# A small clear of an unused tile ahead of every indirect scatter on the queue of GpSimd, with a reordered preparation and a rewritten last layer norm

## The reference

```
x = x + layernorm(attn_block(layernorm(x)))
x = x + layernorm(moe(layernorm(x)))

attn_block: rms_norm, q/k/v, normalised q and k, 16 heads of 8, bias by distance bucket,
            causal softmax, Wo, residual, rms_norm, relu(z @ W1) @ W2, residual
moe:        probs = softmax(x @ router_w.T) over 8 experts; top 2 of them
            h = silu(x @ gate_w[e].T) * (x @ up_w[e].T)        # 352 wide
            y = sum over the token's 2 experts of  prob_e * (h @ down_w[e].T)
layernorm:  (x - mean) / sqrt(var + 1e-5)
```

## Time and profile before

| | |
|---|---|
| median of 3 runs | 629.49 us (626.6 to 630.55) |
| the profiled execution | 628.14 us |
| its span, first to last instruction | 626.1 us |
| PE busy | 544.4 us (87%) |
| ACT, DVE, POOL busy | 391.5, 377.7, 321.9 us |
| granted clock of PE, mean | 0.95 |

### The profile page before, as it was taken

How to read it: one execution, slowest core, us unless ns; L and a number is a source line. 1 busy time by engine, 2 the same in 40 slices (tenths; PEclk the granted TensorE clock), 3 DMA queues, 4 the chain that set the end, 5 groups by cost and what they waited for, 6 DMA issues and landing times.

```text
span 626.1 us, 13770 instructions
## 1 busy us (share of the span) xinstructions
PE 544.4 (87%) x4607; PEld 399.1 (64%) x4607; DVE 377.7 (60%) x1083; ACT 391.5 (63%) x865; POOL 321.9 (51%) x336
## 2 busy tenths in 40 slices
PE   7987899899998998997998999499758689999992
PEld 5763456456565554654565667489658689999950
DVE  6636484966966849988668866227434146555335
ACT  3458899888878888778888774244423144544415
POOL 4023546555458875278955472633454734444426
PEclk9887999999999999999999999889998789999997
DMA  8765323213223332135356212210213102321064
GB/s 198 106 140 135 102 76 120 79 33 102 77 87 101 98 104 76 41 118 131 122 159 147 66 37 54 57 31 15 61 56 85 53 27 69 90 60 31 21 268 135
DMA packets 48117, 55.86 MB, mean 89 GB/s; under 512 B 7821, under 2 KB 42384, under 8 KB 45889
## 3 DMA queue, kind: packets, MB, share of 16 engines
q1 hardware_dynamic: 43728, 46.52, 27.4%
q0 software_dynamic: 4320, 8.47, 4.3%
HBM read 37.12 MB, written 18.29 MB: 89 GB/s over the span
## 4 chain that ended last, share of the span: by engine, by line
PE 60%; DVE 15%; ACT 9%; issue 5%; another core or an unknown queue 5%; POOL 2%; DMA 2%; DVEq 1%; ACTq 0%; POOLq 0%; SPq 0%
PE SC L814 13%; PE OA L688 9%; PE OA L824 8%; PE M L729 5%; PE M L765 4%; ACT arena L933 4%; PE SC L670 3%; PE SC L674 2%; DVE SS L1220 2%; PE M L604 2%; PE SC L680 2%; PE M L623 1%; PE M L654 1%; PE M L795 1%
## 5 line engine op out<-in xcount | busy, mean ns | idle before, releaser
L933 ACT ACTIVATE arena<-SC 128x1024 f32<-128x1024 f32 x160 | 161.7, 1039 | 13.2 <-PE SC L675 11.0
L814 PE MATMUL SC<-arena 128*128 128x128 f32 (+1 forms) x852 | 111.4, 283 | 0.9 <-DVE arena L1401 0.9
L814 PEld LDWEIGHTS SC<-arena 128*128 128x128 f32 (+1 forms) x852 | 104.0, 191 | 1.4 <-DVE arena L1401 1.1
L1620 POOL DMA_INDIRECT slots<-XBA,IDX x64 | 71.9, 1123 | 56.4 <-DVE IDX L1345 39.6
L688 PE MATMUL OA<-arena 128*32 128x256 f32 (+1 forms) x1536 | 90.7, 355 | 5.4 <-DVE arena L410 2.8
L1393 DVE TENSOR_TENSOR arena<-arena,SC 128x256 f32<-128x256 f32 (+1 forms) x142 | 43.7, 348 | 84.6 <-remote 26.9
L824 PE MATMUL OA<-arena 128*128 (+1 forms) x426 | 64.2, 289 | 31.4 <-DVE arena L1393 12.5
L824 PEld LDWEIGHTS OA<-arena 128*128 128x128 f32 (+1 forms) x426 | 56.4, 202 | 34.5 <-issue 34.5
L1626 POOL DMA_INDIRECT ytok<-YSA,XGA x39 | 38.7, 992 | 61.0 <-ACT YSA L1036 57.0
L688 PEld LDWEIGHTS OA<-arena 128*32 128x32 f32 x1536 | 39.4, 110 | 44.4 <-issue 23.0
L409 POOL TENSOR_TENSOR arena<-arena 128x512 f32<-128x512 f32 x32 | 42.6, 1332 | 35.1 <-ACT arena L933 34.5
(11 more groups left out here) (220 smaller groups left out, 1063.9 us busy)
## 6 DMA issues: line engine op xcount, KB each, us to landing
arena<-parts SPq DMA_DIRECT2D x90, 192.0 KB
parts<-arena SPq DMA_DIRECT2D x16, 384.0 KB
arena<-ytok SPq DMA_DIRECT2D x8, 512.0 KB, 6.9
XGA<-slots SPq DMA_DIRECT2D x39, 65.0 KB
arena<-slots SPq DMA_DIRECT2D x32, 65.0 KB
X<-in_L_attn_x SPq DMA_DIRECT2D x4, 512.0 KB, 5.1
arena<-toe SPq DMA_DIRECT2D x16, 128.0 KB, 6.1
out<-X SPq DMA_DIRECT2D x8, 256.0 KB, 2.3
```

What stands on the lines that cost most here:

```text
L814: mm = pe.matmul(SC[0:n, r % 2, 512 * m + P * c:512 * m + P * (c + 1)], WSEL[s % 4][:, I * m + i0:I * m + i0 + n], XGT[r % 2], start=True, ...
L933: act.activation(EB[u], SC[:, n % 2, :], ACT.Exp).then_inc(exp_done, 1)
L1620: pool.indirect_dma_start(out=slots_d.ap(), out_offset=bass.IndirectOffsetOnAxis(ap=IDX[b // 2 % 2][:, k, T * r + t:T * r + t + 1], axis=0 ...
```

## The change

1. `put` and, for the last four batches, `scatter` issue `pause()` ahead of each indirect DMA: POOL clears IDLE, a tile of 128x128 float32 that nothing reads, and waits for that by `link`. That is one clear for each of the 71 puts, ahead of the wait for its result, and one for each of 32 scatter DMAs.
2. Preparation: `spread_cm` multiplies all 128 rows (CMW, cleared by DVE first) in place of 16; ACT takes the exponential of CF ahead of `xar(1)` and that of the first half of the table ahead of the last copy of batch 1; there are fewer dummy matmuls.
3. Last stage: PE adds the halves of 5 batches only, POOL of batches 1 and 4, DVE of batch 7. The inverse root starts from a logarithm and an exponential on ACT (`final_seeds`) and gets one Newton step on POOL, for the last two batches on DVE. Residuals and stores are dealt out in another order.

```diff
+        IDLE = sb("IDLE", [P, P])
+        CMW = EB[UNITS - 1][:, 3 * P:4 * P]
...
+        BY_POOL, BY_VECTOR = (1, 4), (7,)
+        BY_TENSOR = [b for b in range(NB) if b not in BY_POOL + BY_VECTOR]
+        OUT_POOL, OUT_VECTOR = (0, 1, 2, 4), (3, 7, 5, 6)
...
-            for b in (*range(NB - 2), NB - 1, NB - 2):
+            for b in (0, 1, 3, 2, 4, 7, 5, 6):
                 store(sp, b)
...
-                    mm = pe.matmul(CMB[:, h, :], IDN[0:H, h:h + 1].broadcast_to([H, P]), CMR[:, :], start=True, stop=True)
+                    mm = pe.matmul(CMB[:, h, :], IDN[:, h:h + 1].broadcast_to([P, P]), CMW, start=True, stop=True)
...
             for i in range(2):
-                keep_busy(3)
+                keep_busy(2)
                 pre_qk(1, i)
-            keep_busy(5)
+            keep_busy(2)
...
-            for b in range(NB):
+            for b in BY_TENSOR:
                 pe.wait_ge(yt_in[b], 16)
...
-            xar(1)
-            for k in range(3):
-                pre_copy(1, k)
             act.wait_ge(bias_in[0], 16 * (P // COPIES + 1))
             act.activation(CF[:, :], CF[:, :], ACT.Exp).then_inc(tab_exp, 1)
+            xar(1)
+            for k in range(2):
+                pre_copy(1, k)
             exp_table(0)
+            pre_copy(1, 2)
...
+            act.preload_act_table_set("natural_log_exp_and_others")
+            def final_seeds(q):
+                y = RSR[:, 0, 2 * T * q:2 * T * (q + 1)]
+                act.wait_ge(f_stat, 2 * q + 2)
+                act.activation(y, MV[:, 2 * T * q:2 * T * (q + 1), 1], ACT.Ln, bias=FEPS[:, 0:1]).then_inc(f_seed, 1)
+                act.wait_ge(f_seed, 2 * q + 1)
+                act.activation(y, y, ACT.Exp, scale=-0.5).then_inc(f_seed, 1)
...
+            final_seeds(0)
+            final_norm(0)
+            final_seeds(1)
+            final_norm(1)
+            final_norm(2)
+            final_seeds(2)
+            final_norm(3)
+            final_norm(4)
+            final_seeds(3)
+            final_norm(5)
+            final_norm(6)
...
+            dve.memset(CMW, 0.0)
...
                 for k in range(2):
+                    if b >= NB - 4:
+                        pause()
                     pool.indirect_dma_start(out=slots_d.ap(), out_offset=bass.IndirectOffsetOnAxis(ap=IDX[b // 2 % 2][:, k, T * r + t:T * r + t + 1], axis=0),
                                             in_=XB[r][:, t, k, :], in_offset=None).then_inc(scattered[r], 16)
+            def pause():
+                link(pool.memset(IDLE[:, :], 0.0))
             def put(s, r):
+                pause()
                 pool.wait_ge(ys_rdy, s + 1)
...
-                link(pool.tensor_scalar(y, MV[:, pair, 1], 1.0, LN_EPS, ALU.mult, ALU.add))
-                pool.tensor_scalar(nm, MV[:, pair, 0], -1.0, None, ALU.mult)
-                link(pool.tensor_tensor(y, y, MH[:, :], ALU.pow))
+                pool.tensor_scalar(nm, MV[:, pair, 0], -1.0, None, ALU.mult)
+                pool.tensor_scalar(h, MV[:, pair, 1], -0.5, -0.5 * LN_EPS, ALU.mult, ALU.add)
+                pool.wait_ge(f_seed, 2 * q + 2)
+                link(pool.tensor_tensor(u, y, y, ALU.mult))
+                link(pool.tensor_tensor(u, u, h, ALU.mult))
+                link(pool.tensor_scalar(u, u, 1.5, None, ALU.add))
+                link(pool.tensor_tensor(y, y, u, ALU.mult))
                 pool.tensor_tensor(nm, nm, y, ALU.mult).then_inc(f_rstd, 1)
```

More of the change, by code:

```diff
@@ L1535, in residual, with add_pair, moments @@
                 dve.tensor_tensor(x1, x1, FY[b][:, 0], ALU.add).then_inc(f_out[0], 1)
-            for b in range(NB):
-                dve.wait_ge(sum_full, b + 1)
+            def add_pair(b):
+                dve.wait_ge(yt_in[b], 16)
+                link(dve.tensor_tensor(FY[b][:, 0], FY[b][:, 0], FY[b][:, 1], ALU.add))
+            def moments(b):
+                if b in BY_TENSOR:
+                    dve.wait_ge(sum_full, BY_TENSOR.index(b) + 1)
+                elif b in BY_POOL:
+                    dve.wait_ge(f_sum, BY_POOL.index(b) + 1)
                 for t in range(T):
-                    last = dve.bn_stats(ST[:, T * b + t, :], SUMS[b][:, P * t:P * (t + 1)])
+                    last = dve.bn_stats(ST[:, T * b + t, :], summed(b, t))
                 link(last)
@@ L1544, in _ @@
                 last.then_inc(f_stat, 1)
-                if b >= 3 and b % 2:
-                    residual(b - 3)
-            dve.wait_ge(f_rstd, NB // 2)
+            for b in range(NB - 2):
+                moments(b)
+            add_pair(NB - 1)
+            moments(NB - 2)
+            moments(NB - 1)
+            residual(OUT_VECTOR[0])
+            pair = slice(T * (NB - 2), T * NB)
+            y, a, u = RSR[:, 0, pair], NWC[:, 0:2 * T], NWA[:, 0:2 * T]
+            dve.wait_ge(f_stat, NB)
+            link(dve.tensor_scalar(a, MV[:, pair, 1], LN_EPS, None, ALU.add))
+            dve.wait_ge(f_seed, NB)
+            link(dve.tensor_tensor(u, y, y, ALU.mult))
+            link(dve.scalar_tensor_tensor(u, u, -0.5, a, ALU.mult, ALU.mult))
+            link(dve.scalar_tensor_tensor(y, u, 1.5, y, ALU.add, ALU.mult))
+            dve.scalar_tensor_tensor(NM0[:, 0, pair], MV[:, pair, 0], -1.0, y, ALU.mult, ALU.mult).then_inc(f_rstd, 1)
             for t in range(T):
                 i = T * (NB - 1) + t
-                last = dve.tensor_scalar(FY[NB - 1][:, 0, t, :], SUMS[NB - 1][:, P * t:P * (t + 1)], MV[:, i, 0:1], RSR[:, 0, i:i + 1],
+                last = dve.tensor_scalar(FY[NB - 1][:, 0, t, :], FY[NB - 1][:, 0, t, :], MV[:, i, 0:1], RSR[:, 0, i:i + 1],
                                          ALU.subtract, ALU.mult)
@@ L1554, in _ @@
             dve.tensor_tensor(x1, x1, FY[NB - 1][:, 0], ALU.add).then_inc(f_out[0], 1)
-            residual(NB - 2)
+            for b in OUT_VECTOR[2:]:
+                residual(b)
         @block.gpsimd
@@ L1677, in residual, with add_pair, final_root @@
                 pool.tensor_tensor(x1, x1, FY[b][:, 0], ALU.add).then_inc(f_out[1], 1)
[L1679 removed]
+            def add_pair(b):
+                pool.wait_ge(yt_in[b], 16)
+                pool.tensor_tensor(FY[b][:, 0], FY[b][:, 0], FY[b][:, 1], ALU.add).then_inc(f_sum, 1)
+            def final_root(q):
                 pair = slice(2 * T * q, 2 * T * (q + 1))
                 y, nm = RSR[:, 0, pair], NM0[:, 0, pair]
+                h, u = FNW[:, 0, :], FNW[:, 1, :]
                 pool.wait_ge(f_stat, 2 * q + 2)
[L1683 removed]
                 pool.tensor_scalar(nm, MV[:, pair, 0], -1.0, None, ALU.mult)
[L1685 to L1689 removed]
+                pool.tensor_scalar(h, MV[:, pair, 1], -0.5, -0.5 * LN_EPS, ALU.mult, ALU.add)
[4 more added lines that the diff above has]
+                link(pool.tensor_tensor(y, y, u, ALU.mult))
+                pool.tensor_tensor(nm, nm, y, ALU.mult).then_inc(f_rstd, 1)
+            add_pair(BY_POOL[0])
+            final_root(0)
+            add_pair(BY_POOL[1])
+            final_root(1)
+            residual(OUT_POOL[0])
+            final_root(2)
+            for b in OUT_POOL[1:]:
+                residual(b)
 _INS = ['L0_attn_x', 'L0_attn_ln1_w', 'L0_attn_Wq', 'L0_attn_Wk', 'L0_attn_Wv', 'L0_attn_rel_bias', 'L0_attn_scale',
```

23 lines of the change are left out of this document (13 added, 10 removed).

## The result

| | before | changed |
|---|---|---|
| median of the runs, us | 629.50 (626.60 to 630.55) | 618.21 (618.17 to 621.50) |
| profiled execution, span, us | 626.1 | 616.4 |

The ratio is 0.9856, with a 95% interval of 0.981 to 0.9902. The change is faster, by 11 us or 1.4%. I had forecast 594: the direction is right and the time is within the wide range of 585 to 622, but the gain is a third of the 36 us that I had summed.

The account below looks back on a forecast made before the run. PE held 60% of the chain, with 31.3 us lost to late semaphores. Gains of 32 + 2.3 + 1.4 = 35.7 us off 628.14 gave 592.4, with 1.35 added 593.8, stated as 594; range 585 to 622 (0.80).

Parts of the forecast that it names:

- the holes: Between 395 and 503 us the chain waits 31.3 us for late semaphores, while POOL issues indirect DMAs 1.27 us apart.
- the second rival: The clear does not touch the cause, the holes stay and only 3.7 us go: 625.8 us, chance 0.13.
- The first rival: Spacing of 1.45 us is too tight, semaphores pass late half the time: 19.3 us gained, 606.5 us, chance 0.14.
- The clock: Sign to look for in the changed profile: PE's granted clock at 1.0 from 375 us on.
- the pauses: Clears ahead of POOL's indirect DMAs in the tile stage end the late semaphores: 32 us gained, between 0 and 38.6.
- the preparation: Shorter spread matmuls and an earlier table exponential before the first scores: 2.3 us gained, between 0 and 4.
- The last eight scatters: Issued around tile 27, they take 11.6 us; tile 40, which needs their rows, is 27 us off, so not late.
- the price of a put: On POOL, clear and wait make back-to-back DMAs 0.97 + 0.20 + 0.28 = 1.45 us apart instead of 1.27.
- POOL does not bound the stage.: In the tile stage the clears fit POOL's idle time ahead of puts: no cost, at most 0.2 us at the last.
- The 1.44 us a DMA: Each indirect DMA on POOL holds something for 1.44 us, read from three strings; closer ones build a backlog.
- Last stage: After the last put, DVE does the last root itself with seeds from ACT: 1.4 us gained, between 3 gained and 1.5 lost.
- The third rival: Clears hold up DVE's weight copies in the tiles, 71 x 0.20 = 14.2 us longer: 640 us with no cure, chance 0.07.

Follow-up runs that it names:

- no_pauses: The changed kernel without any clear, preparation and last stage still changed; 626.60 us, ratio 0.998 to the kernel before.
- lag_256: The changed kernel with 128x256 clears for scatters and puts, a put's clear waited for only by the next clear; 611.52 us, ratio 0.9704 to the kernel before.
- wide_448: The changed kernel with 128x448 cleared ahead of each put after the first, waited for only by the next clear; 598.36 us, ratio 0.9554 to the kernel before.
- Experiment 3: The changed kernel with a bounds check, as the puts have, added to the scatters; 636.65 us in one execution.
- wide_512_busy: The changed kernel with 128x512 put clears waited for only by the next clear, and 24 instead of 14 idle matmuls after the last tile; 599.13 us, ratio 0.9573.
- bounds_on_scatter: The changed kernel with a bounds check on the scatters, which no index exceeds; 636.65 us in one execution.
- pauses_on_before: The kernel before with the clears alone, old preparation and last stage; 622.82 us, ratio 0.9936 to the kernel before.

## Why the prediction was right and wrong

**Right: the cause of the holes.** Long rows of indirect DMAs 1.27 us apart hold the other engines' semaphores up, and a pause between them is a cure. All 31.3 us of holes went, the second rival ("the holes stay") fell, and `no_pauses` shows that it was the clears. The first rival ("half a cure") fell with some luck: it was about a spacing of 1.45, and the puts stood 1.96 apart. At 1.46 (`lag_256`) 14.0 us of holes remain. The clock did not stay at 1.0 from 375 us on, as I had written: over 16 us around 492 its mean is 0.68. But TensorE waits there for the first rows behind the last scatter, not in a hole; more of this below.

```profile
484.00:500.00 16.00, 7.67 (x42) 7.27 (x41) 3.50 (x9) 2.98 (x12) 10.98 (x18) 0.68 0.21 59
```

**Nearly right: what TensorE gains, and a wait that I had at nothing.** I took 32 us for the pauses and 2.3 for the preparation, 34 for TensorE's end. It gained 27.4 (593.2 to 565.8). Up to tile 38 it had gained more than I forecast: that tile was evacuated at 523.47 before and at 486.05 now, 37.4 us earlier. Then it stood still:

```profile
523.47 0.37 ACT L1036 ACTIVATE YSA<-OA,XGA 128x128 f32<-128x128 f32 x1 [0.79 <-issue]
...
486.05 0.36 ACT L1050 ACTIVATE YSA<-OA,XGA 128x128 f32<-128x128 f32 x1
...
493.87 0.47 PE L819 MATMUL M<-IDN,arena 128*128 128x128 f32 x1 [8.06 <-DMA arena<-slots]
```

"The last eight scatters, issued around tile 27 ... tile 40 ... is 13 x 2.11 = 27 us off. Neither is late" was wrong. Before, the last scatter was at 497.48, when ScalarE had evacuated 28 tiles. Now it is at 488.84, only 8.6 us earlier, and 38 tiles were out: TensorE had run ahead of the scatters, and SP, which loads no row of tile 40 before they have landed, waited 17.4 us for them. TensorE idled 8.06 us, and its clock was at the lower level behind that. By tile 40 the gain was down to 26.8 us (527.96 to 501.16). The kernels without a hole in the chain all have this wait, 5.5 us or more.

`wide_448` had 29.1 us less from the start of the tiles to their end (190.9 against 220.0), so that is nearer to what the pauses can bring with this wait left in. The changed kernel had 24.5 (195.5): its last scatter came 118.6 us after the start of the tiles, against 114.7 in `wide_448`. That its scatters stand in one queue with the slower puts is the likely reason, and no run tested it by itself.

**The step that failed: the price of a put.** "Where DMAs stood back to back, the spacing becomes 0.97 + 0.20 + 0.28 = 1.45 us." For scatters that is so, 1.47. The 0.28 came from a scatter, which has no bounds check; the put has one, and 0.77 us stands behind its clear. Experiment 3 shows the check to be the cause. I said nothing of it, though the code has `bounds_check` in the one and not in the other, and the gap of 0.77 us stood in the trace of the kernel before.

**And with it: "POOL does not bound the stage."** "At the even pace the clear and its wait, 0.48 us, lie in the 1.14 us of idle time ahead of each put ... Cost nothing, at most 0.2 us should the last put slip." That idle time is there only because POOL had caught up: in the kernel before it works off the puts that waited for the last scatters at 1.28 us each, while TensorE makes one in 2.11. At 1.96 to 2.12 it does not catch up, and the idle time of the earlier trace rows never comes to be. I priced the clears in a steady state that they prevent. The term was 0 to 0.2 us; it measured 18.1 - 1.3 = 16.7 us. My own list of what would prove me wrong named strings at 1.45 beside a slow pace, and not a row that is never worked off.

**The 1.44 us a DMA** was too low for rows of puts: holes of 9.0 us remain at 1.49 and none at 1.62. The earlier trace rows shows when ACT was released behind three strings; that this time divided by the number of DMAs is what each DMA needs was a guess that three equal quotients made look like a measurement. Had the put's clear cost what I thought, the nearest run is `lag_256`, with puts 1.46 and scatters 1.57 apart: 611.5 us, not 594. The first rival's 606.5 was nearer.

**Preparation.** The last twelve spread matmuls took half, as forecast, and the first exponential of a body came at 41.04, 2.4 us earlier than before (43.47); "before 42 us" held. Timeline of the changed kernel, which answers to the earlier trace rows:

```profile
28.51 1.50 PE L659 MATMUL SC<-arena,IDN 128*128 128x128 f32 x12
...
37.43 2.77 ACT L1064 ACTIVATE arena<-arena 128x3072 f32<-128x3072 f32 x1
...
41.04 1.96 ACT L947 ACTIVATE arena<-SC 128x1024 f32<-128x1024 f32 x2
```

How much of it reaches the tiles can't be told: with the same preparation they started between 368.8 (`wide_512_busy`) and 374.7 us (`bounds_on_scatter`), before at 373.2. At TensorE's last tile nothing of it is to be seen: 566.0 us in `pauses_on_before`, with the old preparation, and 565.8 here.

**Last stage.** I had taken 1.4 us off 30.6. It is 31.6 in the changed kernel, 1.0 longer. With the clock held it is 29.9, and 30.1 in `no_pauses`: the edit gives 0.5 to 0.7, and the wait for the puts takes more than that back. `pauses_on_before`, with the same wait and the old stage, has 32.7, by which the edit gives 1.1.

**The sum, by what the profiles show.** From 626.1 to 616.4 us: start of the tiles -2.9, the tiles on TensorE -24.5, the last put behind TensorE +16.7, last stage +1.0; together -9.7.

**The third rival** (the clear holds up DVE's weight copy) fell: the copy's mean went from 544 ns to 553, 0.6 us over all 71. Rather the copy holds the clear up: clears took 0.46 to 0.53 us in place of 0.22 where they fell into a copy. The Trainium skill (SBUF — State Buffer, "Who interferes with whom") has both directions in its rule: a DVE copy in a two-port mode and a GpSimd instruction exclude each other for the whole instruction, and the first to issue goes ahead. The traces agree in kind. In `wide_448` a clear that started 0.16 us into a copy took 0.76 us in place of 0.49, and a copy that started 0.05 us into a clear took 0.82 in place of 0.53. With wide clears the copy's mean is longer too, 609 to 632 ns.

```profile
L1439 DVE COPY arena<-arena 128x704 f32 x71 | 39.2, 553 | 17.4 <-issue 15.0
```

## What to carry to other kernels

An engine's idle time in the even part of a stage covers a new cost only if the engine still gets there. Ask first how much is waiting when the even part begins, and divide the time left by the number of pieces: here 1.7 us for each of 42 puts, and the change took 2.12. A gain on one engine also brings forward the moment at which it needs what the others have not yet made: here the rows of the last scatters, 8.06 us. A cure by spacing has two ends: the shortest distance that stops the harm (for the long row of puts here between 1.49 and 1.62 us) and the longest that the engine's row allows (1.7); take the duration of a wait from the very kind of instruction that will stand behind it.

## What was not expected of the hardware

- An indirect DMA with a bounds check starts 0.77 to 0.80 us behind an instruction that POOL waits for, one without a check 0.28 us. Where it does not wait for the clear ahead of it, the checked one starts 0.16 to 0.17 us behind it: the register instruction then has time beside the clear, as I read it. Back to back in the kernel before, both kinds start 0.30 us behind the DMA ahead. Behind ScalarE's result the put of the kernel before also starts 0.77 us late.
- Kernels whose puts stand 1.28, 1.35, 1.46 and 1.49 us apart in a row had holes of 42.4, 24.8, 14.0 and 9.0 us in the chain, at 1.62 and above none. Rows of eight scatters at 1.47 us made none. What it is that holds the semaphores up stays open; the runs show only that it goes by the distance of the DMAs or by the clears that make it.
- A 128x640 clear took 0.65 us alone and mostly 0.93 to 0.99 where it met DVE's weight copy, a 128x448 one 0.49 and 0.76.
